# Four engine queues of a routed-expert kernel laid out anew, with two banks for the first product

## What is computed

```python
x = x + tanh(g_xattn[0]) * experts(layernorm(x), token_ids, ctx, ctx, ctx)
x = x + tanh(g_ffn[0]) * low_rank(layernorm(x), Wr, br, Wd, bd, Wu, bu)

# experts: 4 experts, each a 512x512 matrix W[e]; a row's token id says which one
g = silu(h @ W[e].T);  u = h @ W[e].T;  y = (g * u) @ W[e].T
# low_rank: 8 small experts of rank 16, the best 2 by softmax of the logits
logits = h @ Wr + br + bonus
w      = top-2 gates, normalised
out    = sum_e w[e] * (relu(h @ Wd[e] + bd[e]) @ Wu[e] + bu[e])
```

## Time and profile before

| | |
|---|---|
| median of 3 runs (lowest, highest) | 239.81 us (238.13, 240.24) |
| the profiled execution | 238.26 us |
| its span | 236.5 us |
| busy: PE, DVE, ACT, POOL | 77%, 59%, 51%, 49% |
| mean granted TensorE clock | 0.938 |

### The profile page before, as it was taken

The page is one execution under the profiler, slowest core; times in us unless marked ns, Lnnn a source line. Parts: engine busy times, 40 slices in busy tenths (PEclk is TensorE's granted clock), DMA queues, the critical chain, the costliest instruction groups (busy, mean ns, idle before and its releaser), DMA issues.

```text
span 236.5 us, 5853 instructions
## 1 busy us (share of the span) xinstructions
PE 181.9 (77%) x1558; PEld 119.6 (51%) x1559; DVE 140.0 (59%) x452; ACT 121.8 (51%) x254; POOL 115.6 (49%) x261
## 2 busy tenths in 40 slices
PE   1767978789999887888698787889869985835550
PEld 1746953546666555464455645556456562413310
DVE  5778837576766665757656565545755745444421
ACT  2875893983476645628365473654734535401200
POOL 3678443536155837455473534534446446422421
PEclk9999997999999999999999999999999999597655
DMA  5947751323139343331333313343134032120111
GB/s 178 355 110 259 160 124 39 94 47 84 55 87 136 78 99 98 88 91 44 89 85 95 89 44 91 70 110 89 44 89 99 34 89 49 41 81 8 44 44 44
DMA packets 43028, 21.62 MB, mean 91 GB/s; under 512 B 38632, under 2 KB 38760, under 8 KB 43008
## 3 DMA queue, kind: packets, MB, share of 16 engines
q1 hardware_dynamic: 40448, 12.99, 23.5%
q0 software_dynamic: 2560, 8.39, 11.1%
HBM read 9.06 MB, written 4.19 MB: 56 GB/s over the span
## 4 chain that ended last, share of the span: by engine, by line
POOL 28%; issue 26%; PE 15%; DVE 14%; DVEq 9%; ACT 4%; ACTq 2%; DMA 1%; POOLq 1%
POOL rs L501 6%; POOL xs L483 4%; DVEq L1229 4%; DVEq L1230 3%; POOL neg_mean L567 3%; POOL half_second L540 3%; PE ps_aT L682 3%; POOL mrs L502 3%; POOL ve L500 2%; DVE xs L1236 2%; POOL half_first L538 2%; ACT dev L870 2%; DVE w_rep L1289 2%; DVE w_lo L1096 2%; POOL hot_slot L476 2%
## 5 line engine op out<-in xcount | busy, mean ns | idle before, releaser
L682 PE MATMUL ps_aT<-hT,w_hi 128*128 128x128 f16 x304 | 64.8, 228 | 1.7 <-DVE prod L1212 1.0
L683 PE MATMUL ps_aT<-hT,w_hi 128*128 128x128 f16 x304 | 63.4, 223 | 0.0
L684 PE MATMUL ps_aT<-hT,w_lo 128*128 128x128 f16 x304 | 63.3, 223 | 0.0
L682 PEld LDWEIGHTS ps_aT<-hT,w_hi 128*128 x304 | 30.0, 99 | 15.1 <-issue 4.1
L658 PE MATMUL ps_y<-w_hi,pT_hi 128*128 x76 | 30.3, 399 | 2.4 <-DVE w_lo L1096 1.9
L1236 DVE SCALAR_TENSOR_TENSOR xs<-ps_y,y_t,xs 128x512 f32 x19 | 14.3, 751 | 30.2 <-issue 27.1
L683 PEld LDWEIGHTS ps_aT<-hT,w_hi 128*128 x304 | 30.5, 100 | 1.3
L660 PE MATMUL ps_y<-w_hi,pT_lo 128*128 x76 | 30.3, 399 | 0.0
L684 PEld LDWEIGHTS ps_aT<-hT,w_lo 128*128 x304 | 30.0, 99 | 0.6
L659 PE MATMUL ps_y<-w_lo,pT_hi 128*128 x76 | 30.2, 397 | 0.0
L870 ACT ACTIVATE dev<-xs,neg_mean 128x512 f32<-128x512 f32 (+1 forms) x15 | 10.8, 722 | 30.1 <-POOL neg_mean L567 30.1
(11 more groups left out here) (217 smaller groups left out, 424.8 us busy)
## 6 DMA issues: line engine op xcount, KB each, us to landing
w_nat<-in_ctx_dram SPq DMA_DIRECT2D x4, 1024.0 KB, 7.6
xs<-in_x_dram,rows_of POOLq DMA_INDIRECT x16, 3.6
wd_nat<-in_L_ffn_Wd_dram SPq DMA_DIRECT2D x4, 64.0 KB
wu_nat<-in_L_ffn_Wu_dram SPq DMA_DIRECT2D x1, 256.0 KB
hT<-h_parts SPq DMA_TRANSPOSE x16, 2.7
out_dram<-xs,rows_of POOLq DMA_INDIRECT x16, 2.9
h2T<-h_parts SPq DMA_TRANSPOSE x15, 2.8
b_in<-in_L_ffn_bd_dram SPq DMA_DIRECT2D x1, 64.0 KB
```

The source lines that it names most:

```text
L682: mm(ps_aT[:, n, :], hi, hT[:, q, kc, :], start=(kc == 0), stop=False)
L683: mm(ps_aT[:, n, :], hi, hT[:, q, KC + kc, :], start=False, stop=False)
L684: last = mm(ps_aT[:, n, :], lo, hT[:, q, kc, :], start=False, stop=(kc == KC - 1))
```

## The change

The pipeline gets deeper by one step for the low-rank half: step i now does `hidden_product` to `weigh` of tile i-7 and `transpose_weighted` to `rows_out` of tile i-8; `neg_mean` to `h2_low` stay at tile i-5. What is kept between those stages has two buffers each. One tile more is therefore left for the tail: its transposes and low-rank products are those of tiles 11 to 15 where they were 12 to 15, and its hidden products those of 12 to 15 where they were 13 to 15. The last tile uses banks of its own in the tail.

The first product alternates between two banks, ps_aT[0] and ps_aT[1], and waits for `product` of two pairs back. `neg_mean` moves from POOL to ACT. `choice` is two operations on POOL where it was five; the comparison with the expert numbers is one DVE operation on both choices (`picked`), and the factor half_s is applied in `weighted_high` and `weighted_low`. The register loads of `add_y` (DVE) and `normalize` (ACT) stand at the head of the step. In POOL's queue the gathers, the choice and `rows_out` come ahead of the `rstd` of rows just gathered. The order of the rest in each step is in the diff.

```diff
...
             def choice(k):
-                pool.wait_ge(arg_done, k + 1)
-                then(g.tensor_copy(arg8f[:, :], arg8[:, :]))
-                if k:
-                    pool.wait_ge(w8_done, k)
-                g.tensor_scalar(half_first[:, :], slot_no[:, 0:EF], arg8f[:, 0:1], half_s[:, :],
-                                  ALU.is_equal, ALU.mult)
-                then(g.tensor_scalar(half_second[:, :], slot_no[:, 0:EF], arg8f[:, 1:2], half_s[:, :],
-                                       ALU.is_equal, ALU.mult))
-                g.tensor_tensor(half_sum[:, :], half_first[:, :], half_second[:, :], ALU.add)
-                g.tensor_tensor(half_dif[:, :], half_first[:, :], half_second[:, :],
-                                  ALU.subtract).then_inc(mix_done, 1)
+                q = k % 2
+                pool.wait_ge(picked_done, k + 1)
+                if k > 1:
+                    pool.wait_ge(w8_done, k - 1)
+                g.tensor_tensor(both[:, q, :], picked[:, q, 0, :], picked[:, q, 1, :], ALU.add)
+                g.tensor_tensor(differ[:, q, :], picked[:, q, 0, :], picked[:, q, 1, :],
+                                ALU.subtract).then_inc(mix_done, 1)
...
+            def rstd_of_rows(k):
+                pool.wait_ge(dev_done, k + 1)
+                rstd(1, neg_mean[:, k:k + 1], 1.0, dev_sq[:, k:k + 1], 1.0 / D, k, rstd2)
+            for i in range(-4, NP):
...
+                if i > -4:
+                    gather(i + 4 + AHEAD)
+                if 0 <= i - 2 - LATE:
+                    rstd_of_rows(i - 2 - LATE)
+                if 0 <= i - 4 - LATE:
+                    choice(i - 4 - LATE)
+                if 0 <= i - 5 - LATE:
+                    rows_out(i - 5 - LATE)
                 if 0 <= i + 4 < T:
                     pool.wait_ge(aggr1, i + 5)
                     rstd(0, mv1[:, 0:1], -1.0, mv1[:, 1:2], 1.0, i + 4, rstd1)
                 if i == -4:
                     pairs_tiles()
-                gather(i + 4 + AHEAD)
-                k = i - 3 - LATE
-                if 0 <= k < T:
-                    choice(k)
-                k = i - 4 - LATE
-                if 0 <= k < T:
-                    rows_out(k)
+                    gather(AHEAD)
+            rstd_of_rows(T - 2)
+            choice(T - 4)
+            rows_out(T - 5)
+            pool.wait_ge(aggr2, 1)
+            rstd(1, mv2[:, 0:1], -1.0, mv2[:, 1:2], 1.0, T - 1, rstd2)
+            choice(T - 3)
+            rows_out(T - 4)
+            choice(T - 2)
+            choice(T - 1)
+            rows_out(T - 3)
+            rows_out(T - 2)
+            rows_out(T - 1)
...
-                        mm(ps_aT[:, n, :], hi, hT[:, q, kc, :], start=(kc == 0), stop=False)
...
+                        mm(ps_aT[q][:, n, :], hi, hT[:, q, kc, :], start=(kc == 0), stop=False)
...
-                    wait_last(pe, prod_done, i)
+                    if not (isinstance(i, int) and i < 2):
+                        pe.wait_ge(prod_done, i - 1)
                     first_product(i, q, e_now, range(0, KC // 2))
-                if some(T, -4 - LATE, i0):
-                    transpose_weighted(i - 4 - LATE)
+                if some(T, -5 - LATE, i0):
+                    transpose_weighted(i - 5 - LATE, (i0 - 5 - LATE) % 2)
                 if has_a:
                     first_product(i, q, e_now, range(KC // 2, KC)).then_inc(a_done, 1)
+                if some(T, -4 - LATE, i0):
+                    hidden_product(i - 4 - LATE, (i0 - 4 - LATE) % 2)
+                if some(T, -5 - LATE, i0):
+                    low_rank_out(i - 5 - LATE, (i0 - 5 - LATE) % 2)
                 if meanwhile:
                     meanwhile()
                 if isinstance(i, int) and i + 1 < ON_PE:
                     transpose_h(i + 1)
-                if some(T, -3 - LATE, i0):
-                    hidden_product(i - 3 - LATE, (i0 - 3 - LATE) % 2)
-                if some(T, -4 - LATE, i0):
-                    low_rank_out(i - 4 - LATE)
                 if has_y:
                     second_product(i - 1, e_last)
...
+            def negative_mean(k):
+                act.wait_ge(x1_done, k + LATE + 1)
+                a(neg_mean[:, col(k)], row_sum[:, col(k)], ACT.Copy, scale=-1.0 / D).then_inc(neg_mean_done, 1)
...
             def step(i, i0, meanwhile=None):
-                early = isinstance(i, int) and i < 2
+                has_h, has_2 = some(NP, 3, i0), some(T - 1, -2 - LATE, i0)
+                if has_h:
+                    tile = tile_of(i + 3)
                 if some(NP, -1, i0):
                     product_high(i - 1)
-                if some(T, -4 - LATE, i0):
-                    weighted_high(i - 4 - LATE)
                 if meanwhile:
                     meanwhile()
-                if some(T - 1, -2 - LATE, i0):
+                if has_2:
+                    negative_mean(i - 2 - LATE)
+                if some(T, -5 - LATE, i0):
+                    weighted_high(i - 5 - LATE, (i0 - 5 - LATE) % 2)
+                if has_h:
+                    normalize(i + 3, (i0 + 3) % 2, tile, not some(T, 3, i0))
+                if has_2:
                     deviations(i - 2 - LATE)
-                if some(NP, 3, i0) and not early:
-                    normalize(i + 3, (i0 + 3) % 2, not some(T, 3, i0))
-                if i0 == 1:
-                    normalize(3, 1, False)
-                if some(NP, 0, i0):
-                    act.wait_ge(a_done, i + 1)
-                    a(silu[:, :, :], ps_aT[:, :, :], ACT.Silu, scale=inv_t[:, col(i)]).then_inc(silu_done, 1)
...
-                if some(T - 1, -2 - LATE, i0):
+                if some(T, -4 - LATE, i0):
+                    tanh_gap(i - 4 - LATE, (i0 - 4 - LATE) % 2)
+                if has_h:
+                    normalize_high(i + 3, (i0 + 3) % 2)
+                silu_of(i, i0 % 2)
+                if has_2:
                     normalize2(i - 2 - LATE)
                     normalize2_high(i - 2 - LATE, (i0 - 2 - LATE) % 2)
...
+                dve.wait_ge(arg_done, k + 1)
...
+                v.tensor_tensor(picked[:, q, :, :], expert_no[:, :].unsqueeze(1).to_broadcast([P, 2, EF]),
+                                arg8[:, q, 0:2].bitcast(i32).unsqueeze(2).to_broadcast([P, 2, EF]),
+                                ALU.is_equal).then_inc(picked_done, 1)
...
-            def step(i, i0, meanwhile=None):
-                early = isinstance(i, int) and i < 2
-                if some(NP, -1, i0):
-                    pT_low(i - 1)
-                if some(NP, 2, i0) and not early:
-                    h_low(i + 2, i0 % 2)
-                if some(T, -4 - LATE, i0):
-                    weighted_low(i - 4 - LATE)
-                if meanwhile:
-                    meanwhile()
-                if some(T, 4, i0) and not early:
+                v.scalar_tensor_tensor(wT_lo[:, q, :, :], wT_bank(k)[:, 0:2, :], half_s[:, :],
+                                       wT_hi[:, q, :, :], ALU.mult, ALU.subtract).then_inc(wtT_lo_done, 1)
...
-                if some(T, -3 - LATE, i0):
-                    hidden(i - 3 - LATE)
+                add_y(i - 1, *where)
+            def step(i, i0):
+                where = place(i - 1)
+                if some(NP, 2, i0):
+                    h_low(i + 2, i0 % 2)
+                if some(T, -5 - LATE, i0):
+                    weighted_low(i - 5 - LATE, (i0 - 5 - LATE) % 2)
+                pT_low(i - 1)
                 if some(T, -4 - LATE, i0):
-                    add_low_rank(i - 4 - LATE)
+                    hidden(i - 4 - LATE, (i0 - 4 - LATE) % 2)
+                if some(T, 4, i0):
+                    statistics1(i + 4)
+                if some(T, -5 - LATE, i0):
+                    add_low_rank(i - 5 - LATE)
+                if some(T, -4 - LATE, i0):
+                    weigh(i - 4 - LATE, (i0 - 4 - LATE) % 2)
+                product(i, i0 % 2)
+                add_y(i - 1, *where)
                 if some(T - 1, -2 - LATE, i0):
                     h2_low(i - 2 - LATE, (i0 - 2 - LATE) % 2)
...
+            where = place(NP - 1)
             pT_low(NP - 1)
-            weighted_low(T - 4)
-            hidden(T - 3)
+            weighted_lo(T - 5)
+            hidden_of(T - 4)
+            add_low_rank(T - 5)
+            weigh_of(T - 4)
+            h2_low(T - 2, (T - 2) % 2)
+            add_y(NP - 1, *where)
+            statistics2_last()
+            weighted_lo(T - 4)
+            hidden_of(T - 3)
             add_low_rank(T - 4)
-            h2_low(T - 2, (T - 2) % 2)
-            weigh(T - 3)
-            add_y(NP - 1, *place(NP - 1))
-            statistics2_last()
-            weighted_low(T - 3)
-            hidden(T - 2)
-            add_low_rank(T - 3)
+            weigh_of(T - 3)
             dve.wait_ge(last_hi, 1)
             q = (T - 1) % 2
             v.tensor_tensor(h2T[:, q, KC:2 * KC, :], ps_h2T[:, :, :], h2T[:, q, 0:KC, :],
                             ALU.subtract).then_inc(last_lo, 1)
```

(13 more changed lines are left out.)

299 lines of the change are left out of this document (171 added, 128 removed).

## The result

The changed kernel takes 205.65 us (median of 4 runs, 205.06 to 205.84) against 239.25 for the kernel before (4 runs on the same chip): a ratio of 0.859, with a 95% interval of 0.855 to 0.864, so 14% faster. Forecast was 215.5 with a range of 210 to 225. The profiled execution took 205.47, its span is 203.7. Two executions further down, 197.51 us of a_const and 221.88 us of b_early_loads, are slow ones at a lower clock: the medians contain them, the ratios don't.

A forecast was written before the change was run, and what follows sets the result against it. The prediction took the loop as bound by latency and order, a turn of hand-overs between engines. 173.4 us to A(18) plus 38.8 of tail gave a 212.2 span; with 1.76 around it and a median adjustment, 215.5 us, range 210 to 225.

The forecast's parts named there:

- The turn as the bound: Main loop: a 10.19 us round of hand-overs between engines sets the step; both TensorE waits are ends of it.
- TensorE alone 8.39: Main loop: one step without a TensorE wait, A(17) to A(18), taken as what TensorE needs alone, 8.39 us.
- I take 8.5: Ten steps up to A(18): 8.5 us each assumed, a tenth above the step without a wait.
- Rival 3: TensorE's edge met everywhere, early rows lose nothing: 8.3 us a step, tail 37, 210.5 us; chance 12%.
- Register loads of VectorE: VectorE's step: loads cost 1.6 us each before, about 0.55 behind h2_low, bounds 0 and 1.6.
- Banks: First product's second bank: worth at most the single 1.0 us wait for product; without it late silu blocks A.
- GpSimd and its port: GpSimd beside VectorE: no loss taken, 2 us as bound; by the skill's blocking rule 2 to 3 us longer.
- Steps 3 to 6: Early steps: y(3) 1 us late, about 0.5 in steps 5 and 6; net 0.5 late at A(7), 81.1.
- The tail: From A(18) to the span's end: 38.8 us where it was 47.55, giving 8.7, bounds 3 and 11.

The follow-up runs named there:

- a_const: The changed kernel with expert 0's weights for every pair on TensorE, so that no expert register is loaded or used there; 195.75 us.
- b_early_loads: The kernel before with VectorE's two register loads moved to the head of its step, nothing else; 219.62 us, ratio 0.914.
- b_const: The kernel before with expert 0's weights for every pair on TensorE, so no expert register there; 235.57 us.
- a_early_pT: The changed kernel with pT_low ahead of the register loads and of h_low on VectorE in steps 1 to 6; 202.61 us.
- b_warm_tail: The kernel before with 45 added matmuls of 512 columns, read by nobody, put where TensorE waits in the tail; 233.28 us.
- a_one_bank: The changed kernel with the first product in one bank instead of two; 215.55 us.
- best1: a_unroll_carry with pT_low first in steps 1 to 6, second-layer weight work behind it, and tile 1's rstd ahead of a gather; 191.63 us.
- a_unroll: The changed kernel with TensorE's loop of two steps a pass written out for pairs 8 to 18; 202.34 us.
- a_unroll_carry: The changed kernel with TensorE's loop written out and one expert register load a step there instead of two; 196.41 us.
- a_late_loads: The changed kernel with VectorE's two register loads put back directly ahead of the addition of y; 206.43 us.

## Why the prediction was right, and where it was wrong

The direction and the bound that was to go were right. The time was not: it lies under the range, and the step of the working that failed is the one on TensorE's own pace. The span was forecast at 212.2 and is 203.7. The 8.5 us divide into +0.9 before A(8), -5.7 in the ten steps and -3.7 in the tail.

**The turn as the bound: right.** Both waits of TensorE left the loop together, and b_const shows that 0.75 us less of TensorE's busy time a step (74.5 us in the ten steps, 82.0 before) buys nothing while the turn stands. What I didn't see is the second turn of some 8.4 us behind it, which the depth and the order had to pass as well.

**"TensorE alone 8.39", "I take 8.5": the step that failed.** I took a step without a wait for the least that TensorE needs. It was one step at the queue's pace, with A's second half at 0.24 us a triple and a lead of 0.28 us in the first. The changed kernel gets the lead back in every second step (from A(12) on, steps of 7.6 and 8.2 alternate, 7.93 in the mean), and without register work the step needs 7.07. Rival 3 had the right direction, but its 8.3 a step still lies above the 8.18 us of busy time, and the busy time contained the queue's pace. The register rows of TensorE stood in the trace of before as well, and I hadn't read them.

**Register loads of VectorE: size about right, weight wrong.** I expected 0.55 behind h2_low; the row ahead of h_low shows 0.54 in the step at 131 us, and 5.6 us over 10 times. But I listed them among the edits that come with the new order. By themselves they give 19 us under the old order, and under the new one 0.8.

**Banks: wrong.** "It is worth at most that", 1.0 us, agrees with the old order (1.3 us by the medians, within the noise). In the new order the bank is worth 9.9 us. I had named that silu would be in A's way and put no price on it.

**GpSimd and its port: the bound wasn't needed.** In the ten steps GpSimd waits 30.1 us for ScalarE's deviations, so a loss there would be hidden. Its powers beside a working VectorE:

```profile
L516 POOL TENSOR_TENSOR rs<-ve,neg_half x15: 550/567/1118, 89.2 to 164.6; 128x1 f32<-128x1 f32 x15
```

At least one of the 15 took double, 0.55 us more, and half of them took 0.57 or less. The rule of the Trainium skill (SBUF — State Buffer, "Who interferes with whom") that I weighed could be at work there; of its 2 to 3 us on the sum the loop shows nothing.

**Steps 3 to 6: right in kind.** y(2), y(3) and y(5) waited 0.58, 0.76 and 0.35 us for pT_lo, A(7) started at 81.98 (forecast 81.1) and A(8) at 89.28 (88.4). a_early_pT shows the price of that order, 2.2 us.

**The tail: mis-sized by 3.7.** y(18) came 10.2 us after A(18) (11.3 forecast), its addition 5.4 later (5.7), the last low-rank addition 13.7 after that (16.5), the end 5.8 later (5.3):

```profile
178.78 0.39 PE L677 MATMUL ps_y<-w_hi,pT_hi 128*128 x1 [1.92 <-DVE pT_lo L1331]
...
184.19 0.75 DVE L1314 SCALAR_TENSOR_TENSOR xs<-ps_y,y_t,xs 128x512 f32 x1
...
197.86 0.75 DVE L1344 SCALAR_TENSOR_TENSOR xs<-ps_aT,out_coef,xs 128x512 f32<-128x512 f32 x1
```

These answer to the earlier trace rows. I had let the clock recover for y(18) and kept 0.65 for what follows; it was 0.89 there. b_warm_tail puts 6.2 us on the clock in the old order. normalize2 of tile 15 started 0.04 us after its rstd's last operation, as forecast. In the new order the clock of this stretch differs from run to run of this set, and its length goes with it: from y(18) on 23.8 to 24.0 us at 0.96 or more (a_early_pT, a_one_bank, best1), 24.9 at 0.89 or 0.90 (the changed kernel, a_const, a_unroll), 25.6 and 26.2 at 0.83 and 0.82 (a_unroll_carry, a_late_loads, the last with its loads bare).

Not tried: the old order with the loads behind h2_low, which would divide its second turn; the new order's clock held low with nothing else changed; what the loop's branch costs without its register work; and what raised the tail's clock in the changed kernel from 0.73 to 0.92.

## What to carry to other kernels

A step in which an engine never waits is not its floor: read the distance between the starts of its instructions, and the register operations in its queue, before you take busy time for need. Ask of each piece of a turn what the next turn behind it is: here three cheap edits each hit the same second turn, and of the kernels run only those with the new order passed it. Once TensorE is the bound, look at register loads and register-addressed small matmuls on its own queue first.
